# Norm ahead of the head weights' powers, first query splits in the projection's block, and one block less

## What is computed

```
x = x + _L0_attn_ref(_layernorm(x, axis=-1), w_qkv, w_proj, q_gamma, q_beta, k_gamma, k_beta)
x = x + _L0_xattn_ref(_layernorm(x, axis=-1), ctx_768, Wq, bq, Wkv, bkv, Wo, bo)
...
# _L0_attn_ref, 16 heads of 16 columns
qkv = (x @ w_qkv).reshape(B, S, 3, H, Dh)
...
q = _layernorm(q, q_gamma, q_beta)
k = _layernorm(k, k_gamma, k_beta)
logits = jnp.einsum('bhsd,bhtd->bhst', q, k) / (math.sqrt(Dh) * T)
att = jax.nn.softmax(logits, axis=-1)
```

## Time and profile before

| | us |
|---|---|
| median of 3 runs | 1850.25 |
| lowest and highest | 1847.56 and 1850.53 |
| the profiled execution's own time | 1847.56 |
| its span | 1845.8 |
| TensorE, VectorE, ScalarE, GpSimd busy in it | 1685.6, 1578.3, 1381.8, 324.8 |

### The profile page before, as it was taken

The page is one execution under the profiler, slowest core; times in us unless marked ns, Lnnn a source line. Parts: engine busy times, 40 slices in busy tenths (PEclk is TensorE's granted clock), DMA queues, the critical chain, the costliest instruction groups (busy, mean ns, idle before and its releaser), DMA issues. The chain is left out here.

```text
span 1845.8 us, 38826 instructions
## 1 busy us (share of the span) xinstructions
PE 1685.6 (91%) x15155; PEld 699.9 (38%) x15155; DVE 1578.3 (86%) x2295; ACT 1381.8 (75%) x2670; POOL 324.8 (18%) x591
## 2 busy tenths in 40 slices
PE   5899989999999999998999999999989998779993
PEld 3542222332332233223322222222235555657872
DVE  5798999989989998987899999999948886768877
ACT  3529989889889988997899899998975654534543
POOL 4801011211021111111101000010014444300002
PEclk9899999999999999999999999999999999889995
DMA  4000000000000000200000000000011000000001
GB/s 134 1 1 1 2 1 1 2 1 2 2 2 1 2 2 1 93 2 1 2 2 1 2 2 2 1 2 2 2 32 51 1 1 1 1 1 1 1 1 46
DMA packets 12450, 18.64 MB, mean 10 GB/s; under 512 B 1840, under 2 KB 10544, under 8 KB 12016
## 3 DMA queue, kind: packets, MB, share of 16 engines
q1 hardware_dynamic: 11568, 14.79, 2.5%
q10 hardware_dynamic: 704, 1.38, 0.2%
HBM read 14.07 MB, written 2.10 MB: 9 GB/s over the span
## 5 line engine op out<-in xcount | busy, mean ns | idle before, releaser
L935 DVE TENSOR_REDUCE mxp<-ps_m 128x2 f32<-128x1024 f32 (+1 forms) x960 | 1088.6, 1187 | 92.5 <-PE ps_m L712 91.4
L861 ACT ACTIVATE work<-ps_s 128x512 f32<-128x512 f32 x1856 | 1010.8, 599 | 132.8 <-PE ps_s L725 84.7
L739 PE MATMUL ps_av<-work,vst 128*32 128x256 f32 x7424 | 595.4, 392 | 11.7 <-ACT avs L868 11.1
L725 PE MATMUL ps_s<-qb,k_stack 50*128 50x512 f16 x1856 | 364.7, 382 | 31.6 <-ACT work L861 25.5
L712 PE MATMUL ps_m<-k_stack,qa 48*128 48x512 f16 (+1 forms) x2048 | 370.7, 359 | 6.4 <-DVE mxp L935 3.4
L739 PEld LDWEIGHTS ps_av<-work,vst 128*32 128x32 f32 x7424 | 147.3, 108 | 346.1 <-ACT work L861 259.4
L725 PEld LDWEIGHTS ps_s<-qb,k_stack 50*128 50x128 f16 x1856 | 109.5, 92 | 423.0 <-ACT work L861 406.8
L712 PEld LDWEIGHTS ps_m<-k_stack,qa 48*128 48x128 f16 x2048 | 105.2, 94 | 44.0 <-DVE mxp L935 33.1
L570 POOL TENSOR_SCALAR mtmp<-negm 128x16 f32<-128x16 f32 x32 | 8.2, 255 | 530.9 <-DVE negm L940 530.7
L1477 PE MATMUL pbank<-k_stack,pxh 128*128 128x512 f16 x128 | 48.6, 380 | 5.8 <-ACT pscaled L1623 3.3
L2372 DVE TENSOR_TENSOR opl<-ops_p,oph 128x512 f16<-128x512 f32 x64 | 36.0, 585 | 20.9 <-ACT oph L2289 20.9
(11 more groups left out here) (401 smaller groups left out, 2109.8 us busy)
## 6 DMA issues: line engine op xcount, KB each, us to landing
x_res<-in_x SPq DMA_DIRECT2D x4, 512.0 KB, 8.1
w_experts<-in_w_experts SPq DMA_DIRECT2D x1, 2048.0 KB, 7.8
out<-x_res SPq DMA_DIRECT2D x8, 256.0 KB, 2.1
v_rows<-in_ctx_c SPq DMA_DIRECT2D x1, 1664.0 KB, 11.7
work<-in_ctx_t SPq DMA_DIRECT2D x1, 1456.0 KB, 16.1
ctx_n<-in_ctx_n SPq DMA_DIRECT2D x1, 1248.0 KB, 7.3
w_qkv<-in_w_qkv ACTq DMA_DIRECT2D x1, 768.0 KB, 9.1
w_qkv<-in_w_qkv SPq DMA_DIRECT2D x1, 768.0 KB, 4.2
```

Source lines behind the costliest of these rows:

```text
L725: pe.matmul(ps_s[:, banks[e], :], STACKS[part(n)][rows, pair, keys], qb[n % 2][rows, j, :, :], start=True, stop=True).then_inc(s["sc"], 1)
L739: m = pe.matmul(ps_av[32 * h:32 * h + 32, cols], vst[n % 2][:, t, h, :], pbuf[(tau[n] + t) % 2][:, h, cols], start=(t == 0 and half == 0), ...
L861: a.activation(pbuf[g % 2][:, h, :], ps_s[:, b, :], ACT.Exp, scale=factor).then_inc(s["exp"], 1)
L935: v.tensor_reduce(dst, src, AX.X, ALU.max).then_inc(s["mred"], 1)
```

## The change

1. On VectorE `powers()` moves from in front of `statistics(0)` to behind `centre()`, still in front of `statistics(2)`.
2. The tiles `qnat` and two semaphores are made outside the attention block. The split of the first two groups of queries (with the clearing of the rest of `qnat`) moves into the projection block: VectorE does it in steps n = 16 and n = 17, behind `key_out`, after a wait for the queries of the first four tiles. The function is now `split_queries`, the same three instructions.
3. `end_load` goes. GpSimd, TensorE, ScalarE and VectorE wait for the semaphore of the loads themselves in the attention block, where they first need one.
4. `AHEAD_KV` goes: TensorE starts with the two turns of queries, and all 52 context quarters go between the 40 units.

```diff
@@ attentions @@
-    AHEAD_KV = 1
-    QUARTERS = [(j, half, k) for j in range(AHEAD_KV, TM) for half in range(2) for k in range(2)]
+    QUARTERS = [(j, half, k) for j in range(TM) for half in range(2) for k in range(2)]
...
         @block.gpsimd
         def _(g):
+            g.wait_ge(*loaded)
...
-            for j in range(AHEAD_KV):
-                for half in range(2):
-                    for k in range(2):
-                        context_quarter(j, half, k)
             turn_q(0)
             turn_q(1)
+            pe.wait_ge(*loaded)
             for g in range(EARLY):
...
-            for j in range(AHEAD_KV):
-                context(j)
             ev(qa[0])
             ev(qa[1])
-            for j in range(AHEAD_KV, TM):
+            a.wait_ge(*loaded)
+            for j in range(TM):
                 context(j)
...
+            v.wait_ge(*loaded)
             c(v.tensor_scalar(bq[:, :], bq[:, :], 0.25, None, ALU.mult))
-            for p in range(2):
-                v.memset(qnat[p][:, :, :, MAXROWS:HALF], 0.0).then_inc(s["qset"], 1)
-                queries(v, p)
@@ new @@
+QSPLITS = 3
+def split_queries(eng, qn, qnat, block, group, done, base):
+    c = Counted(eng, done, base)
+    src = qn[:, block * QC:block * QC + QC, group * GW:group * GW + GW].rearrange("p t (h d) -> p t h d", d=HD)
+    for i in range(2):
+        c(eng.tensor_copy(qnat[:, :, :, i * HD:(i + 1) * HD], src))
+    c.wait()
+    c(eng.tensor_tensor(qnat[:, :, :, 2 * HD:3 * HD], src, qnat[:, :, :, 0:HD], ALU.subtract))
+    assert c.n == QSPLITS, c.n
+    c.wait()
@@ self_qkv @@
-            powers()
             statistics(0)
             statistics(1)
             norm_front(0)
             head_sums()
             norm_back(0)
             centre()
+            powers()
             statistics(2)
             for n in range(STEPS):
...
                 if 0 <= n - LAG - 1 < T:
                     key_out(n - LAG - 1)
+                if 0 <= n - T < 2:
+                    v.wait_ge(s["aff"], 4 * QC)
+                    v.memset(qnat[n - T][:, :, :, MAXROWS:HALF], 0.0).then_inc(s_qset, 1)
+                    split_queries(v, qn, qnat[n - T], 0, n - T, s_qsplit, QSPLITS * (n - T))
@@ decoder @@
+            qnat = [sb(cs, f"qnat{p}", [P, QC, HG, HALF], F16) for p in range(2)]
+            s_qset, s_qsplit = fresh(prog, "qset"), fresh(prog, "qsplit")
...
-            end_load(prog, (s_cross, 16 * len(cross_in)))
```

More of the change, by code:

```diff
@@ L345, in attentions @@
                spare, valid, ones, ident, identh, later, we, weh, wel, gain,
-               ctx_c, kh, kl, ctx_gain, ctx_t, wkv):
+               ctx_c, kh, kl, ctx_gain, ctx_t, wkv, qnat, s_qset, s_qsplit, loaded):
     nc = prog["nc"]
@@ L365, in attentions @@
     assert len(KEY_TURNS) == TM
-    QS, MS, LNS, CHAIN = 3, 3, 20, 10
-    s = {k: fresh(prog, k) for k in ("set", "qset", "qsplit", "mx", "mred", "negm", "msplit", "sc", "exp", "vst", "av",
+    MS, LNS, CHAIN = 3, 20, 10
+    s = {k: fresh(prog, k) for k in ("set", "mx", "mred", "negm", "msplit", "sc", "exp", "vst", "av",
                                      "avev", "rc", "kpeak", "diag", "chain", "kh", "kl", "kset", "st", "ln", "pw", "xr", "late", "wchain", "ctx")}
@@ L443, in attentions @@
     EARLY = due(0)
-    AHEAD_KV = 1
-    QUARTERS = [(j, half, k) for j in range(AHEAD_KV, TM) for half in range(2) for k in range(2)]
+    QUARTERS = [(j, half, k) for j in range(TM) for half in range(2) for k in range(2)]
     units, made = 3 + TM, EARLY
-    qa_at, qb_at, scored, o_at, x_at, k_at = {0: AHEAD_KV + 1, 1: AHEAD_KV + 2}, {0: TM + 3}, {}, {}, {}, {}
+    qa_at, qb_at, scored, o_at, x_at, k_at = {0: 1, 1: 2}, {0: TM + 3}, {}, {}, {}, {}
     settled_at, proj_at, query_at, peak_done, spread_done = {}, {}, {}, 0, 0
@@ L486, in sb @@
             return cx.enter_context(nc.sbuf_tensor(f"{name}_{prog['n']}", shape, dt))
-        qnat = [sb(f"qnat{p}", [P, QC, HG, HALF], F16) for p in range(2)]
         qa = [sb(f"qa{p}", [P, PAIRS, QC, P], F16) for p in range(3)]
@@ L520, in queries @@
                 eng.wait_ge(s["mred"], query_at[block_of(n) * QC + QC - 1])
[L521 to L528, removed]
+            split_queries(eng, qn, qnat[n % 2], block_of(n), group(n), s_qsplit, n * QSPLITS)
         @block.sync
@@ L563, in shifts @@
                 g.wait_ge(s["negm"], n + 1)
-                g.wait_ge(s["qset"], 2)
-                g.wait_ge(s["qsplit"], n * QS + QS)
+                g.wait_ge(s_qset, 2)
+                g.wait_ge(s_qsplit, n * QSPLITS + QSPLITS)
                 c = Counted(g, s["msplit"], n * MS)
@@ L667, in turn_q @@
             def turn_q(n):
-                pe.wait_ge(s["qsplit"], n * QS + QS)
+                pe.wait_ge(s_qsplit, n * QSPLITS + QSPLITS)
                 turn(n)
@@ L1042, in _, with self_qkv @@
             v.wait_ge(s["mred"], taken[0])
-def self_qkv(prog, x, st, mean, rstd, tmp, w, gain, shift, undo, qn, kn, v_nat, ks, ident, identb, identh, loads, x_in, beside):
+QSPLITS = 3
[8 more added lines that the diff above has]
+    c.wait()
+def self_qkv(prog, x, st, mean, rstd, tmp, w, gain, shift, undo, qn, kn, v_nat, ks, ident, identb, identh, qnat, s_qset, s_qsplit, loads, x_in, beside):
     nc = prog["nc"]
@@ L2657, in decoder @@
                 s_cross = nc.alloc_semaphore("cross_in")
-                self_qkv(prog, x, st, mean, rstd, tmp, w, gain, shift, undo, qn, kn, v_nat, ks, ident, identb, identh,
+                self_qkv(prog, x, st, mean, rstd, tmp, w, gain, shift, undo, qn, kn, v_nat, ks, ident, identb, identh, qnat, s_qset, s_qsplit,
                          ((ident[:, :], a["ident"]), (gain[:, :, :], a["gain"]), (shift[:, :, :], a["shift"]),
@@ L2668, in decoder @@
                         (ctx_c, rows2(a["ctx_c"]))],
-                       we, weh, wel, expert_gain, ctx_c, kh, kl, ctx_gain, ctx_t, wkv)
+                       we, weh, wel, expert_gain, ctx_c, kh, kl, ctx_gain, ctx_t, wkv, qnat, s_qset, s_qsplit, (s_cross, 16 * len(cross_in)))
         recycle(prog)
```

## The result

The median went from 1850.3 us to **1871.55 us** (four runs: 1853.39, 1866.24, 1876.86, 1877.88). The ratio to before is 1.0099, 95% interval 1.0071 to 1.0128: slower, by 18.3 us in the interval's middle, where 5.4 us less were predicted. The profiled execution is the quickest of the four: 1853.39 us, span 1851.5 against 1845.8.

What follows compares the result with a forecast made beforehand. VectorE was taken to pace the attention block's opening, with TensorE nearly full; changes in the first 95 us should reach the end unchanged. Terms -5.2 + 2.7 - 0.4 - 2.5 = -5.4 us gave 1844.9 us from 1850.25, range 1841.3 to 1848.4.

Steps and rivals of the forecast that it cites:

- the head: Projection block's start: with powers behind the norm, head sums start at 11.55 instead of 16.74; -5.2 us, bounds -5.5 to -4.2.
- margin: Projection block: GpSimd's scalings end at 20.8, 0.9 us before their first use at 21.65, so nothing was charged.
- the tail and the block's end: Projection block's end: two splits lengthen VectorE's chain by 2.7 us (2.2 to 3.2); dropping the waiting block saves 0.4.
- the first two reductions: Attention block's start: first reduction at B + 3.0, second at B + 4.8 instead of B + 7.27; gain 2.5 us (0.7 to 3.1).
- B: The start of the attention block, 87.00 us in the kernel before.
- the opening's term: Attention block's start without context matmuls in front: 2.5 us gained, with the clock up and VectorE pacing after the second reduction.
- two more units at the low clock: Lower bound of the opening's gain: two more units at 2.0 us each against 1.13, leaving 0.7 us.
- rival 4: Opening: TensorE's clock stays at 1.2 GHz, units take 2.0 us; over 15 units about 1858 us; chance 0.05.
- 4.7 us of work were enough before, and TensorE is nearly as full here: Argument against rival 4: in the kernel before, the clock rose near 91.7, after 4.7 us of TensorE work.
- the quarters are hidden: Opening: four added quarters cost TensorE 1.7 us against 2.4 to spare, so nothing; at most 1.7 without that cover.
- The sum of the steps: Whole change: head -5.2, tail +2.7, block end -0.4, attention start -2.5, together -5.4 us.

Runs made afterwards that it cites:

- the second trace: The changed kernel run once more, unchanged, for a second profile: median 1877.49 us (5 runs), ratio 1.0146 to the kernel before.
- the head alone: The kernel before with only the powers moved behind the centring: 1843.89 us (5 runs), ratio 0.9966.
- the tile in front: The changed kernel with the first context tile's four quarters back ahead of the query turns: 1845.93 us (11 runs); with splits also in VectorE's waits 1844.54 and 1843.79.
- the tile behind the turns: The changed kernel with the first context tile's four quarters unbroken behind the two query turns, ahead of the units: 1845.78 us (11 runs), ratio 0.9984.
- adding two matmuls a unit: The changed kernel with two unread fp16 matmuls behind the quarters of each of the opening's first eight units: 1848.10 us (12 runs), ratio 0.9994.
- the order of the quarters alone: The kernel before with only the context tile ahead removed, all 52 quarters between the 40 units: 1880.70 us (5 runs), ratio 1.0173.
- 14 executions of 16: The changed kernel, context tile in front and query splits in VectorE's waits, run in two series: 1844.54 us (9 runs) and 1843.79 us (7 runs).
- the three versions with the waits filled to the block's start: The changed kernel with unread matmuls in TensorE's tail waits: 1841.67 us; with splits in VectorE's waits too: 1840.03; with ten more matmuls at the first scores: 1837.20.

## Why the prediction was wrong

**Right: the head.** "Taken: -5.2 us": the head sums came 5.45 us earlier, the key copy of tile 13 5.0 (76.09 against 81.08; 5.9 in the second trace, 75.21), the head alone 6.4 +/- 2.4 us in time. Scalings over at 20.5 (20.8 forecast), margin 1.34 us (0.9).

**Right: the tail and the block's end.** Splits 1.53 + 1.00 = 2.5 us (1.60 + 1.08), the slower one again where GpSimd adds; last key copy ending at 83.75 (83.6); 0.53 us from there to TensorE's start in the next block in place of 0.93. By the rule of the Trainium skill (SBUF — State Buffer, section "SBUF: two separate sides") the first split could have taken up to 2.05 us, an estimate with VectorE blocked for the whole of GpSimd's addition. Its two casts took 0.95 us where the others took 0.42: 0.53 us lost beside an addition of 0.92, somewhat over half of it.

**Right: the first two reductions.** B + 2.84 (3.0, though its own terms, 1.03 + 1.07 + 2 x 0.39, add up to 2.9) and B + 4.54 (4.8).

**Wrong: the opening's term, by one sentence.** "By then the clock should be up, as it was before, and VectorE paces again." It was not up, for 11 units in the profiled run and for all 40 in most. The bound I had put to this, "two more units at the low clock", should have been 40. The mechanism was listed as rival 4 with its price right (2.0 us a unit; measured 78.1 / 40 = 1.95) and its chance, 0.05, far too low. The argument against it was "4.7 us of work were enough before, and TensorE is nearly as full here". The runs show what is wrong with it. Fullness by busy time does not raise the clock: 10.00 of 10 at 0.50 for 78 us. What the 4.7 us were made of does matter: four quarters and sixteen turns without a pause raised it, judged by the times, in 25 of 27 runs of the changed kernel with the tile in front, and in all eleven with the tile behind the turns, while quarters in alternation with maxima raised it late (after 23 us in one trace, 62 in another) or not within the 40 units (three traces). That the units run at full clock later was no evidence either: the alternation held a clock that was up in every trace, and did not bring up, in time, one that was down.

**Right: the quarters are hidden**, once the clock is up (9.81 of 10, VectorE 10.00).

The sum of the steps, -5.4 us, was met at the second reduction (-5.45) and lost behind it. That it was met to 0.1 us is luck: in the second trace of the same kernel that reduction comes 6.3 us earlier than before (87.95). Whether the maxima's short rows, the fp32 quarters or the small pauses between the pieces of a unit keep the clock down was not separated; the runs show only that adding two matmuls a unit is enough.

## What to carry to other kernels

Where a block starts with TensorE at 1.2 GHz, find in the trace which unbroken stretch of matmuls raises the clock, and treat it as work with a job: splitting it into the gaps of another engine's pace can cost more than it frees, here 30 us by the order of the quarters alone, for a stretch of 3.75. Read the granted clock beside the busy time, since a full busy share can hide it: a unit with one quarter filled 1.69 us of TensorE at 0.50, and 0.95 at 1.00 (tile in front). Where TensorE waits ahead of such a block, unread matmuls in the waits, down to the last one, kept the clock here and cost no time that these runs show. That, with VectorE's splits moved into its waits, turned a change that lost 27 us into one that gains 8, and 12 with ten more of them at the first scores.

## What the runs showed of the hardware

The granted clock stayed at 0.50 for some 80 us under a TensorE that the records of the units show busy without a gap (10.00 of 10 us). Of the two traces of the changed kernel one has the rise 23 us behind the block's start, the other not before the opening's end; what makes the difference is not shown. That it is a clock and not a mistake of the record is seen in the durations, 1.22 us for a quarter at 0.50 and 0.70 at 1.00. The Trainium skill (TensorE: Matmul & The Clock Gate, section "Part 1: The HAM clock gate") calls the cost of the low start under 1% of a typical span and advises against fitting a count of slow matmuls; the order of the quarters alone measured 1.7%, and here the measurement decides. The same section reports that the gate has been seen stuck at a quarter of the clock for over 50 us; the stretches here are as long, but at half the clock, so they are another case.

With identical instructions in front, 5.5 us of unbroken matmuls were followed by the shorter time in 14 executions of 16; the other two took 30 us more, and the trace of one of them has the clock at 0.50 through the opening. A kernel that rests on such a rise can be one with two times; the three versions with the waits filled to the block's start showed one each, their five runs within 2.2, 3.1 and 4.3 us.
